# Second layer norm of a window transformer: mean in the PSUM ring, centring in SBUF, values product in a bank of its own, 49 weight columns in probabilities times values

## The reference, cut to what matters

```
t = (windows of group_norm(x))                    # 2048 windows of 49 tokens, 96 channels
h = ln(t) * s1 + b1
q, k, v = h @ wq + bq, h @ wk + bk, h @ wv + bv    # 12 heads of 8
t = t + softmax(q k^T / sqrt(8)) v @ wo + bo
h = ln(t) * s2 + b2                                # the second norm
t = t + gelu(h @ w1 + b1) @ w2 + b2
x = x + (windows put back)
```

## Time and profile before

| | us |
|---|---|
| median of 3 runs (lowest, highest) | 5688.36 (5684.9, 5694.23) |
| the profiled execution, its own time | 5688.4 |
| span of the profiled execution | 5686.6 |
| PE busy, share of the span | 94% |
| DVE, ACT, POOL busy | 60%, 62%, 62% |
| mean granted clock of TensorE | 0.976 |

### The profile page before, as it was taken

How to read it: one execution, slowest core, us unless ns; L and a number is a source line. 1 busy time by engine, 2 the same in 40 slices (tenths; PEclk the granted TensorE clock), 3 DMA queues, 4 the chain that set the end, 5 groups by cost and what they waited for, 6 DMA issues and landing times.

```text
span 5686.6 us, 229687 instructions
## 1 busy us (share of the span) xinstructions
PE 5342.2 (94%) x97360; PEld 4217.5 (74%) x97360; DVE 3397.2 (60%) x5850; ACT 3542.0 (62%) x5590; POOL 3509.3 (62%) x4814
## 2 busy tenths in 40 slices
PE   6999999999599999999999999999999999999998
PEld 6999999999466666666666666666666666666665
DVE  2333333433267677677676777776677777777773
ACT  3444444444367777777776777777777777777775
POOL 2222222222367777777777777777777777777774
PEclk9999999999689999999998999999999999999996
DMA  4444444444356666666665666666666666666662
GB/s 125 116 121 120 127 121 120 116 125 104 71 126 140 140 140 140 140 140 140 140 140 127 139 139 140 140 140 140 140 140 140 140 140 140 140 140 140 140 140 47
DMA packets 1099823, 740.58 MB, mean 130 GB/s; under 512 B 465428, under 2 KB 1070708, under 8 KB 1098708
## 3 DMA queue, kind: packets, MB, share of 16 engines
q1 hardware_dynamic: 1069620, 687.18, 53.6%
q0 software_dynamic: 29184, 38.71, 3.2%
HBM read 409.02 MB, written 316.46 MB: 128 GB/s over the span
## 4 chain that ended last, share of the span: by engine, by line
PE 61%; issue 7%; DVE 3%; ACT 3%; POOL 0%; ACTq 0%; DVEq 0%; POOLq 0%
PE ps_pv L1121 14%; PE ps_ring L1188 8%; PE ps_s L1075 5%; PE ps_ring L1058 4%; PE ps_xc L1163 4%; PE ps_ring L1049 4%; PE ps_t L1075 4%; PE ps_ring L1180 4%; PE ps_ring L1066 4%; PE ps_ring L1060 2%; PE ps_ring L1059 2%; DVE b_rest L983 2%; ACT b_sq_hi L848 2%; PE ps_ring L1149 2%; PE ps_ring L1067 2%
## 5 line engine op out<-in xcount | busy, mean ns | idle before, releaser
L940 DVE TENSOR_REDUCE b_mx<-ps_s 113x12 f32<-113x588 f32 x1024 | 783.9, 766 | 200.6 <-PE ps_s L1075 200.4
L1121 PEld LDWEIGHTS ps_pv<-b_vd,b_probs_t 128*64 128x64 f32 x24576 | 771.1, 140 | 164.0 <-issue 155.1
L840 ACT ACTIVATE b_probs_t<-ps_t 128x588 f32<-128x588 f32 x1024 | 667.7, 652 | 303.0 <-PE ps_t L1075 302.9
L225 POOL TENSOR_SCALAR xn<-xin,aff 96x896 f32<-96x896 f32 x192 | 173.4, 903 | 1072.2 <-DVE aff L375 1059.5
L1121 PE MATMUL ps_pv<-b_vd,b_probs_t 128*64 128x18 f32 x24576 | 822.5, 213 | 0.3 <-issue 0.3
L746 POOL TENSOR_TENSOR b_mid_lo<-b_mid,b_mid_hi 128x392 fp32r<-128x392 f32 x768 | 788.9, 1027 | 43.3
L410 PE MATMUL ps_conv<-blocks_hi,toep_hi 128*128 128x288 f32 (+2 forms) x2880 | 667.2, 313 | 0.0
L410 PE MATMUL ps_conv<-blocks_hi,toep_lo 128*128 128x288 f32 (+2 forms) x2880 | 654.4, 309 | 0.0
L410 PE MATMUL ps_conv<-blocks_lo,toep_hi 128*128 128x288 f32 (+2 forms) x2880 | 653.7, 308 | 0.0
L801 POOL TENSOR_TENSOR b_outs<-b_y,b_xs 96x392 f32<-96x392 f32 x256 | 316.7, 1237 | 445.2 <-DVE b_y L1021 445.2
L282 ACT ACTIVATE toep_hi<-toep 128x640 fp32r<-128x640 f32 x288 | 197.2, 749 | 632.9 <-PE ps_conv L410 616.7
(11 more groups left out here) (142 smaller groups left out, 12423.3 us busy)
## 6 DMA issues: line engine op xcount, KB each, us to landing
stacked_qk<-b_planes SPq DMA_DIRECT2D x512, 220.5 KB, 2.9
b_q_st<-stacked_qk SPq DMA_DIRECT2D x512, 220.5 KB, 4.3
b_k_st<-stacked_qk SPq DMA_DIRECT2D x512, 220.5 KB, 5.6
toep<-filters_padded SPq DMA_DIRECT2D x96, 936.5 KB, 14.0
stacked_qk<-b_planes SPq DMA_DIRECT2D x512, 147.0 KB, 2.4
stacked_qk<-b_planes SPq DMA_DIRECT2D x512, 73.5 KB, 1.9
b_xs<-x_scratch SPq DMA_DIRECT2D x224, 147.0 KB, 2.8
out<-b_outs SPq DMA_DIRECT2D x224, 147.0 KB, 3.2
```

The costliest lines, as they stand in the source:

```text
L840: act.activation(pt[:, p, 0:HEADS * TOK].rearrange("k (e n) -> k e n", e=2), ps_t[:, :, 0:HPAIR * TOK], ACT.Exp, scale=float(DH) ** -0.5). ...
L940: dve.tensor_reduce(mx[0:rows_q, :].rearrange("q (e m p) -> q e m p", e=2, p=PAIRS)[:, :, :, p], ps_s[0:rows_q, :, 0:HPAIR * TOK].rearrang ...
L1121: ins = pe.matmul(to, pt[:, p, at:at + WS], vd[:, m % VR, p, h, :, :], start=True, stop=True, skip_group_check=True)
```

## The change

1. `mean2` takes the place of the centring product: PE multiplies `t1` by the averaging matrix into a bank of the ring, and no longer waits for `h1_done` there. DVE subtracts that bank from `t1` into a new SBUF tile `xc2`.
2. ACT's two squares, the rounded one first now, and DVE's `h2_hi` and `h2` read `xc2` in place of `ps_xc`.
3. The values product goes to `ps_xc`, without a wait for a bank of the ring, and stands ahead of `var2` on PE. On DVE its two copies stand ahead of `h2_hi` and `h2`. The next strip's centring product waits for `v_done` in place of `h2_done` and `h2_high`.
4. In `USES`, `mean2` is added before `q` and `v` is taken out. So `q` now waits for `t1_done`, `k` for `xc2`, `var2` for `q_done` as before, `w2` for `k_done`, and `w1a` of the next step for `lg2`.
5. L1121 loads 49 weight columns in place of 64 and writes 49 partitions; `ps_pv` is set to 1.0 once at the start, and `pt` loses its padding.

```diff
-                ("q", QKV, "q_done", 1, 1), ("k", QKV, "k_done", 1, 1),
-                ("var2", PROJ, "lg2", 1, 1), ("v", QKV, "v_done", 1, 1),
+                ("mean2", PROJ, "xc2", 1, 1), ("q", QKV, "q_done", 1, 1),
+                ("k", QKV, "k_done", 1, 1), ("var2", PROJ, "lg2", 1, 1),
                 ("w2", MLPS, "y_done", 1, 1)]
...
                 if proj is not None:
-                    square(i, proj, sq2, "xc2", "sq2", "sq2_split")
-                if proj is not None:
-                    square(i, proj, sq2_hi, "xc2", "sq2_high", "sq2_split", used="var2")
+                    square(i, proj, sq2_hi, xc2[:, :], "xc2", "sq2_high", ("sq2_split", "var2"))
+                if proj is not None:
+                    square(i, proj, sq2, xc2[:, :], "xc2", "sq2", ("sq2_split",))
...
+                if proj is not None:
+                    dve.wait_ge(S["mean2"], proj + 1)
+                    after(dve, i, "sq2", proj)
+                    after(dve, i, "h2_high", proj)
+                    after(dve, i, "h2_done", proj)
+                    dve.tensor_tensor(xc2[:, :], t1[:, proj % 2, :], bank(i, s, "mean2")[0:C, 0:NT],
+                                      ALU.subtract).then_inc(S["xc2"], 1)
                 row_max(i, att, 3)
...
-                    dve.tensor_tensor(h2_hi[:, :], ps_xc[0:C, 0:NT], rstd[:, :], ALU.mult).then_inc(S["h2_high"], 1)
+                    dve.tensor_tensor(h2_hi[:, :], xc2[:, :], rstd[:, :], ALU.mult).then_inc(S["h2_high"], 1)
...
-                        to = ps_pv[WS * odd:WS * odd + WS, 0:PAIRS * HEADS * VA].rearrange(
+                        to = ps_pv[WS * odd:WS * odd + TOK, 0:PAIRS * HEADS * VA].rearrange(
...
-                        ins = pe.matmul(to, pt[:, p, at:at + WS], vd[:, m % VR, p, h, :, :], start=True, stop=True,
+                        ins = pe.matmul(to, pt[:, p, at:at + TOK], vd[:, m % VR, p, h, :, :], start=True, stop=True,
...
                     pe.wait_ge(S["t0_split"], qkv + 1)
-                    after(pe, i, "h2_done", qkv - (PROJ - QKV))
-                    after(pe, i, "h2_high", qkv - (PROJ - QKV))
+                    after(pe, i, "v_done", qkv)
...
                     pe.wait_ge(S["t1_done"], proj + 1)
-
-                    pe.wait_ge(S["h1_done"], qkv + 1 if qkv is not None else BATCH * B)
-                    pe.matmul(ps_xc[0:C, 0:NT], cc("center", C), t1[:, proj % 2, :], start=True,
-                              stop=True).then_inc(S["xc2"], 1)
+                    product(i, s, "mean2", cc("average", C), t1[:, proj % 2, :], C, "mean2")
```

More of the change, by code:

```diff
@@ L519, in window_pass @@
         sq2_lo = sb("sq2_lo", [C, NT], F32R)
+        xc2 = sb("xc2", [C, NT])
         lg = sb("lg", [C, NT])
@@ L558, in window_pass @@
                  "h1_done q_ps k_ps v_ps q_high k_high q_done k_done v_done rest_high qk_split s_ps mx_done mt_ps mx_high mx_rest mx_mid mx_split r_ps exp_done "
[L559 removed]
+                 "pv_ps rden_done o_done ot_ps ot_done wo_ps t1_done mean2 xc2 sq2 var2 lg2 rstd2 h2_done w1_ps gelu_done "
                  "w2_ps y_done added out_done sq1_high sq1_split sq2_high sq2_split h2_high h2_split").split()
@@ L841, in exps, with square @@
                                ps_t[:, :, 0:HPAIR * TOK], ACT.Exp, scale=float(DH) ** -0.5).then_inc(S["exp_done"], 1)
[L843 to L848, removed]
+            def square(i, n, dst, src, ready, done, used, scale=1.0):
+                act.wait_ge(S[ready], n + 1)
+                for u in used:
+                    after(act, i, u, n)
+                act.activation(dst[:, :], src, ACT.Square, scale=scale).then_inc(S[done], 1)
             def gelu(i, s, n, m, use):
@@ L999, in step @@
                         S["mx_rest"], 1)
-                if proj is not None:
-                    dve.wait_ge(S["rstd2"], proj + 1)
-                    after(dve, i, "w1_ps", NM * proj)
-                    after(dve, i, "h2_split", proj)
-                    dve.tensor_tensor(h2_hi[:, :], ps_xc[0:C, 0:NT], rstd[:, :], ALU.mult).then_inc(S["h2_high"], 1)
-                if proj is not None:
-                    dve.wait_ge(S["rstd2"], proj + 1)
-                    after(dve, i, "h2_split", proj)
-                    dve.tensor_tensor(h2[:, :], ps_xc[0:C, 0:NT], rstd[:, :], ALU.mult).then_inc(S["h2_done"], 1)
                 if qkv is not None:
@@ L1014, in step @@
                         ins = dve.tensor_copy(vd[r, qkv % VR, :, :, a, 0:DH],
-                                              bank(i, s, "v")[r, 0:PAIRS * C].rearrange("t (p h d) -> t p h d", p=PAIRS,
+                                              ps_xc[r, 0:PAIRS * C].rearrange("t (p h d) -> t p h d", p=PAIRS,
                                                                                         d=DH))
                     ins.then_inc(S["v_done"], 1)
+                if proj is not None:
+                    dve.wait_ge(S["rstd2"], proj + 1)
+                    after(dve, i, "w1_ps", NM * proj)
+                    after(dve, i, "h2_split", proj)
+                    dve.tensor_tensor(h2_hi[:, :], xc2[:, :], rstd[:, :], ALU.mult).then_inc(S["h2_high"], 1)
+                if proj is not None:
+                    dve.wait_ge(S["rstd2"], proj + 1)
+                    after(dve, i, "h2_split", proj)
+                    dve.tensor_tensor(h2[:, :], xc2[:, :], rstd[:, :], ALU.mult).then_inc(S["h2_done"], 1)
                 if mlps is not None:
@@ L1172, in step @@
                 max_rows(i, s, att)
-                if proj is not None:
-                    spread(i, s, proj, "var2", sq2_hi, sq2_lo, "sq2_split", "var2")
                 if qkv is not None:
-                    wait_bank(pe, i, s, "v")
+                    pe.wait_ge(S["h1_done"], qkv + 1)
                     for p in range(PAIRS):
@@ L1179, in step @@
                             t = slice((2 * p + w) * TOK, (2 * p + w + 1) * TOK)
-                            ins = pe.matmul(bank(i, s, "v")[WS * w:WS * w + TOK, p * C:(p + 1) * C], h1[0:C, t],
+                            ins = pe.matmul(ps_xc[WS * w:WS * w + TOK, p * C:(p + 1) * C], h1[0:C, t],
                                             wv[:, :], start=True, stop=True, skip_group_check=True)
                     ins.then_inc(S["v_ps"], 1)
+                if proj is not None:
+                    spread(i, s, proj, "var2", sq2_hi, sq2_lo, "sq2_split", "var2")
                 if mlps is not None:
```

7 lines of the change are left out of this document (4 added, 3 removed).

## The result

| | before | changed |
|---|---|---|
| median of four runs each (lowest, highest) | 5691.3 (5684.9, 5717.11) | 6083.95 (6010.81, 6160.11) |
| ratio, 95% interval | | 1.0585 [1.0506, 1.0665] |
| the profiled execution | 5688.4 | 6048.42 |
| mean granted clock | 0.976 | 0.871 |

Slower by 6%, where I had forecast faster by 1%. The ratio is taken from the faster two of the changed kernel's four runs, because the other two are over 1.5% above the fastest; the medians of all four stand in the ratio 1.069. The changed kernel's runs scatter over 2.5%, those of the kernel before over 0.6%. The busy shares tell nothing of it: PE has risen from 94% to 95%. The reason stands in the row of the clock.

A forecast was written before the change was run, and what follows sets the result against it. The prediction took the dependency ring through POOL, 15.79 us a step, as the bound. It took 34 us from the race, 7 from the ring and 6 at the low clock off 5688, giving 5641 us, range 5500 to 5695.

The forecast's parts named there:

- Slower: the clock: Rival, chance 0.09: PE's waits make TensorE clock falls frequent, each costing 6.5 us; thirty would give 5836 us.
- The ring through POOL is the bound: Window-pass step: dependencies through DVE, PE, ACT and POOL set its 15.79 us; PE's 0.65 us wait is slack.
- 49 columns, 0.28 us a half: Probabilities times values on PE: narrower weight loads save 0.28 us per half, 0.56 a step.
- `h2_hi` stands still until 0.42 us after L792: DVE: with two SBUF inputs, `h2_hi` waits for POOL's L792 and ends 0.42 us later, at 3200.99.
- The race, lost by 0.05 us in seven steps of eight: DVE's `sq2_lo` against POOL's last L746: loses by 0.05 us, except in L761 steps; 31 wins bring 34 us.
- the cases of every second step or more: Rivals where `sq2_lo` goes first more often: every second or third step, 5557 us, chance 0.17; always, 5455 us, 0.12.
- Once the ring has run ahead, POOL is early too, and the next step loses again: After a step in which `sq2_lo` goes first, the next has it behind POOL's L746 again.
- Squares from SBUF unchanged: ACT's two squares reading `xc2` from SBUF: still 0.88 us, 0.05 either way.
- `xc2` 0.55, `k` waits 0.2: DVE's new subtraction takes 0.55 us; PE's `k` waits for it about 0.2 us.
- `w1` as the place of a new wait: PE: 0.2 us of standing still at `w1`; over 0.5 us moved there would show the forecast wrong.
- the steps with L761: One step in eight, where L761 delays POOL by 0.24 us: `sq2_lo` goes first, the step some 15.0 us.
- the loop: Step if `sq2_lo` always goes first: from L987's end over L792, `h2_hi`, PE and back, 14.92 us.

The follow-up runs named there:

- experiment 3: Changed kernel with the fourth exponential ahead of `rstd2`'s two steps on ACT: 5633.93 us, ratio 0.9875; the same with 64 weight columns: 5787.99 us.
- experiment 4: Changed kernel with two more centring matmuls, results overwritten, ahead of `below_max(0)` on PE, ACT's order unchanged: 5675.51 us, ratio 0.9969.
- experiment 2: Changed kernel, centring product ahead of `below_max(0)`: 6143.91 us; plus two matmuls: 6011.86. Cited for columns alone: kernel before with 49 columns, 5668.61 us.
- experiment 6: Onto experiment 3's 49-column kernel: POOL waits for `sq2_lo`, 5644.34 us; later `h2_lo` wait on PE, 5566.47; both, 5514.81; both with 64 columns, 5617.07.
- the fastest kernel: Experiment 3's 49-column kernel plus POOL waiting for `sq2_lo` and PE waiting for `h2_lo` only behind the first two MLP matmuls: 5514.81 us, ratio 0.9678.
- the kernel of experiment 3 with 64 columns: Changed kernel with the fourth exponential ahead of `rstd2` on ACT and 64 weight columns again: 5787.99 us, ratio 1.0143.
- the first of experiment 2: Changed kernel with the first norm's centring product ahead of `below_max(0)` on PE: 6143.91 us.
- the second of experiment 2: Changed kernel with the centring product ahead of `below_max(0)` and two more centring matmuls whose result is overwritten: 6011.86 us, ratio 1.0436.
- the last of experiment 6: The fastest kernel with 64 weight columns in probabilities times values in place of 49: 5617.07 us, ratio 0.9843.
- experiment 5: Changed kernel with `var2` ahead of the values product again on PE: 5910.98 us, ratio 1.0368.

## Why the prediction was wrong

The step that failed is the clock. The sum put it at nothing, and the rival *Slower: the clock* had a chance of 0.09; it measured 498 us. I wrote that "PE stands still for about 1.2 us a step (0.8 at `var2`, 0.2 at `w1`, 0.2 at `k`)" and set against it that "249 steps with such waits had two falls". On this ground the sum had no term for falls. Three things were wrong with this.

- **A wait was missing from the list.** In moving the values product ahead of `var2` I checked its bank and what starts earlier behind it, but not the next thing PE waits for: `below_max(0)`, with the fourth exponential behind `rstd2` on ACT. The trace of the kernel before had the rows for it, as the 0.24 us above show. I had asked what is queued behind the waiting instruction on DVE and POOL, and not on ACT.
- **The total was taken for the place.** The forecast 0.8 at `var2` did not come in most steps (the race was won), and PE's idle share did not grow (4.6% against 5.1%). What is new is the one 0.3 us that lies between dense matmuls and the stretch of scores and PV. Experiments 3 and 4 show that without it the series of falls are gone. I had compared totals, and the total tells nothing of this.
- **The chance.** Each fall cost 5.5 us where I had 6.5: near. That "from nine more on the kernel is slower" held only for the small win that I forecast. With 138 us to spare it takes some 25, and the kernel of experiment 3 with its 27 falls is still faster than the one before. By my own numbers, though, nine were enough, with two already in the trace, and that should have given this rival more than 0.09. Thirty falls, 5836 us, was the worst I priced; there were 94. Nor did any row at hand show that a fall can bring on the next at a spacing of 20.48 us; 71 of the 94 came that way.

The other steps, by the sentences of the prediction:

- *The ring through POOL is the bound*: confirmed. The columns alone save 0.56 us of PE a step and 0.05 us of the step (experiment 2). 
- *49 columns, 0.28 us a half*: a half now takes 1.21 us (3114.59 to 3115.80) to 1.26 us (2407.79 to 2409.05) from start to start, forecast 1.23. Confirmed.
- *`h2_hi` stands still until 0.42 us after L792*: confirmed. The timeline of DVE and of POOL:

```profile
2402.69 0.56 DVE L986 TENSOR_TENSOR b_sq_lo<-b_sq,b_sq_hi 96x392 fp32r<-96x392 f32 x1 [0.40 <-ACT b_sq L848]
...
2405.73 1.66 DVE L1021 TENSOR_TENSOR b_h_hi<-b_xc,b_rstd 96x392 fp32r<-96x392 f32 x1
2407.31 0.55 DVE L1025 TENSOR_TENSOR b_h<-b_xc,b_rstd 96x392 f32<-96x392 f32 x1
```

```profile
2402.73 1.42 POOL L747 TENSOR_TENSOR b_mid_lo<-b_mid,b_mid_hi 128x392 fp32r<-128x392 f32 x1
2404.36 0.84 POOL L789 TENSOR_SCALAR b_planes<-b_rest 96x784 bf16<-96x784 f32 x1 [0.21 <-DVE b_rest L995]
2405.29 1.68 POOL L793 TENSOR_TENSOR b_planes<-b_rest,b_planes 96x784 bf16<-96x784 f32 x1
```

  L1021 ends at 2407.39, L793 at 2406.97: 0.42. I named 1 us as its duration, which was a slip: the start in the earlier trace rows, 3199.33, and my own end, 3200.99, make the 1.66 that it takes.
- *The race, lost by 0.05 us in seven steps of eight*: mis-sized, and with it the term of 34 us. The same rows show it won by 0.04 us: `sq2_lo` starts at 2402.69 and takes 0.56, L747 starts at 2402.73. Of 145 high-level steps up to 5600 us, 84 are 15.0 us long and only 21 are 15.9. That the margin was smaller than what I did not know of four durations was right; the cases of every second step or more deserved the larger chance. A won step took 15.0 us, as forecast for the steps with L761 (and 14.92 for the loop).
- *Once the ring has run ahead, POOL is early too, and the next step loses again*: wrong. Won steps follow each other, up to six in a row. A reason that fits, argued and not tested, is in the POOL row above: L747 takes 1.42 us beside `sq2_lo`, 1.02 otherwise, so a POOL that comes second pays and is not early. The Trainium skill (SBUF — State Buffer, Who interferes with whom) says that whoever comes second waits for the whole of the other. L747 started 0.04 us after `sq2_lo` and so would wait 0.52 us; its duration is 0.40 us longer than usual. The trace agrees that both directions wait, with a somewhat shorter wait.
- *Squares from SBUF unchanged*: 0.53 and 0.51 us where the earlier trace rows had 0.48 and 0.49; the pair takes 0.95 for 0.88. Small, as bounded.
- *`xc2` 0.55, `k` waits 0.2*: L980 takes 0.56, and `q` with `k` 1.77 us where the two took 1.48 before, so 0.3.
- *`w1` as the place of a new wait*: it came, 0.3 us, once the wait ahead of it was gone (experiment 3).

Had the clock stayed as before, the account gives 6048 - 498 = 5550 us, an estimate: below my forecast of 5641 and beside the 5557 of the race won in every second step. That it lies inside my range is no merit of the sum, whose main term was the race lost in seven steps of eight. The chances between the race's cases were off by that, and the sign by the clock.

**What stays open.** Two things. The exponential's wait is there with 64 columns as well (60 us against 60), but the falls are 23 and not 94, and all but two of them stand outside a series. Whether the series need the shorter PV half ahead of the fall, or the 15.0 us step, or less work on PE in all, no run separates. And the new order brings 11 to 33 falls in every kernel of experiments 3, 4 and 6 in which the wait is gone, where the kernel before has two. In the fastest kernel most of them come behind another wait in the same place, for the row maxima. But in the kernel of experiment 3 with 64 columns 16 of the 18 have no wait in the 20 us ahead of them beyond the one at `var2` that the kernel before has too. What is left as their cause there is the order of the products itself; no run takes it apart.

## What to carry to other kernels

When work is moved ahead of a wait to fill it, follow the engine to the next instruction that depends on another engine, and look at what stands in that engine's order before the releaser: an instruction whose input is ready belongs ahead of those that wait. On TensorE, idle time is not slack of one price. Here 0.3 us a step ahead of a stretch of small matmuls cost 7% of the kernel's time (414 of 6048 us), while the kernel before had 0.68 us a step in another place and two falls. So read the granted clock before anything else, and count its falls and their spacing. An idle spot that can't be removed may be worth filling with dense matmuls; here that gave back 373 us. Put a wait at the instruction that reads the operand, not at the group.

## What the runs showed of the hardware that was not expected

- With 0.3 us of idle time in a step of 15 the mean granted clock was 0.871. Without it, it was 0.944 (experiment 3), and with two matmuls that compute nothing in its place 0.953 (experiment 4); the kernel before had 0.976.
- The falls can settle into a pattern: 13.65 us at 1.2 GHz, 6.83 us at 2.4 GHz, for up to twenty steps on end. In the pieces from 3109.5 and 3130 us the high level holds the values product, `w2`, the new wait and the first PV half.
- Kernels whose falls come in such series scatter widely between four runs: 149 us in the changed kernel, 153 in the first of experiment 2. But series are not needed for it: the second of experiment 2 scatters over 145 us with 38 falls, and the last of experiment 6 over 90 with 19. With 132 falls that are mostly short it is 25 us (experiment 5), with the 11 of the fastest kernel 18 us.
- Matmuls added ahead of an idle time that stays went with fewer falls (93 and 38, experiment 2).
- POOL is held up by DVE as DVE is by POOL (L747: 1.42 us in place of 1.02).
